# First loads issued in the order of use with waits of their own, and spare products on TensorE in the first and last passes of a fused four-layer kernel

## What is computed

```
x = L0(x, ctx, ctx)    # 16 query heads of 16, one K/V head, window mask, output product, SiLU gate, RMS norm, minus its token mean
x = L1(x, ctx, idx)    # RMS norms, 16 heads; each token sees 3 neighbours of its index; squared ReLU weights; residual
x = L2(x, ctx)         # self attention, then cross attention, 16 heads of 64, relative position bias, softmax, residuals
x = L3(x, ctx, mask)   # Mamba-2 block (in-projection, 4-tap convolution, SiLU, decayed sums, gate, RMS norm, out-projection), then 8-head cross attention
```

## Time and profile before

| what | value |
|---|---|
| median of 3 runs | 1463.18 us (1457.23 to 1464.12) |
| the profiled execution | 1463.84 us |
| its span, first to last instruction | 1462.0 us |
| TensorE (PE) busy in the span | 1306.4 us (89%) |
| VectorE (DVE), ScalarE (ACT), GpSimd (POOL) busy | 958.3, 779.8, 356.7 us |
| mean granted TensorE clock | 0.956 |
| share of TensorE, VectorE, ScalarE in the chain that ended last | 72%, 19%, 4% |

### The profile page before, as it was taken

The page is one execution under the profiler, slowest core; times in us unless marked ns, Lnnn a source line. Parts: engine busy times, 40 slices in busy tenths (PEclk is TensorE's granted clock), DMA queues, the critical chain, the costliest instruction groups (busy, mean ns, idle before and its releaser), DMA issues.

```text
span 1462.0 us, 26277 instructions
## 1 busy us (share of the span) xinstructions
PE 1306.4 (89%) x9618; PEld 1027.6 (70%) x9618; DVE 958.3 (66%) x1908; ACT 779.8 (53%) x2690; POOL 356.7 (24%) x782
## 2 busy tenths in 40 slices
PE   3667889999999999999999999999999999888755
PEld 2345667877777787778777777877787777776533
DVE  2446567768686867777686768677776868573522
ACT  1133556657565646566575656464665656464411
POOL 1112303232322213132323232131323232302020
PEclk9779999999999999999999999999999999999855
DMA  6700000000000000000000000000000000000000
GB/s 205 282 1 13 3 12 2 17 4 16 4 16 4 9 11 0 20 0 16 4 16 4 16 4 9 11 0 20 0 16 4 16 4 4 4 5 5 4 4 4
DMA packets 23967, 28.65 MB, mean 20 GB/s; under 512 B 2144, under 2 KB 20096, under 8 KB 23424
## 3 DMA queue, kind: packets, MB, share of 16 engines
q1 hardware_dynamic: 23936, 28.24, 6.0%
HBM read 26.11 MB, written 2.13 MB: 19 GB/s over the span
## 4 chain that ended last, share of the span: by engine, by line
PE 72%; DVE 19%; ACT 4%; issue 3%; SPq 1%; DMA 0%; DVEq 0%; POOL 0%; another core or an unknown queue 0%; POOLq 0%; ACTq 0%
PE psum L477 44%; PE psum L471 8%; PE psum L660 4%; DVE small_ L1002 4%; PE psum L641 3%; PE psum L581 3%; DVE sa_p L996 3%; PE psum L693 2%; PE psum L705 2%; PE psum L525 2%; ACT sa_p L798 2%; ACT A L790 2%; DVE ca_p L1010 1%; PE psum L541 1%; PE psum L737 1%
## 5 line engine op out<-in xcount | busy, mean ns | idle before, releaser
L1286 POOL TENSOR_SCALAR small_<-small_ 128x1 f32<-128x1 f32 x112 | 36.0, 321 | 946.7 <-DVE small_ L1014 477.0
L790 ACT ACTIVATE A<-A,small_ 128x128 f32<-128x128 f32 x384 | 148.5, 389 | 91.0 <-DVE small_ L1003 91.0
L471 PE MATMUL psum<-cst,A 128*128 128x128 f32 x672 | 108.8, 289 | 59.1 <-DVE A L1010 36.7
L783 ACT ACTIVATE A<-psum 128x1024 f32<-128x1024 f32 (+2 forms) x112 | 76.5, 683 | 133.6 <-PE psum L471 125.2
L471 PEld LDWEIGHTS psum<-cst,A 128*128 128x128 f32 x672 | 80.6, 147 | 80.2 <-DVE A L1010 41.7
L1175 DVE SCALAR_TENSOR_TENSOR A<-psum,half_cw,A 128x127 f32<-128x127 f32 (+2 forms) x288 | 76.3, 340 | 68.4 <-ACT A L894 68.4
L790 ACT ACTIVATE ca_p<-ca_p,small_ 128x128 f32<-128x128 f32 x256 | 98.8, 394 | 4.9 <-DVE small_ L1003 4.9
L790 ACT ACTIVATE sa_p<-sa_p,small_ 128x128 f32<-128x128 f32 x256 | 98.8, 392 | 0.1
L783 ACT ACTIVATE sa_k<-psum 128x512 f32<-128x512 f32 (+1 forms) x48 | 35.5, 739 | 98.4 <-PE psum L477 53.5
L790 ACT ACTIVATION_READ_ACCUMULATOR A<-A,small_ 128x1 f32 x384 | 72.1, 188 | 0.0
L477 PEld LDWEIGHTS psum<-sa_p,Wsaq 128*128 128x128 f32 x512 | 58.8, 193 | 18.5 <-issue 18.5
(11 more groups left out here) (219 smaller groups left out, 3281.9 us busy)
## 6 DMA issues: line engine op xcount, KB each, us to landing
inT<-in_tokT SPq DMA_DIRECT2D x16, 256.0 KB, 2.7
ctx_in<-in_ctx SPq DMA_DIRECT2D x16, 128.0 KB, 2.1
A<-bias_rows SPq DMA_DIRECT2D x1, 2048.0 KB, 9.3
Wsakv<-in_wsa_kv SPq DMA_DIRECT2D x1, 2048.0 KB, 12.3
Wcakv<-in_wca_kv SPq DMA_DIRECT2D x1, 2048.0 KB, 13.3
ctx_end<-in_tokT SPq DMA_DIRECT2D x16, 128.0 KB, 2.2
out<-x_out SPq DMA_DIRECT2D x16, 128.0 KB, 1.7
Wmi<-in_wm_in SPq DMA_DIRECT2D x1, 1288.0 KB, 18.7
```

What stands on the lines that cost most here:

```text
L471: mm = pe.transpose(out[:, c * P:(c + 1) * P], src[:, c * P:(c + 1) * P], ident)
L783: return act.activation(out, in_, ACT.Copy)
L790: ins = act.activation(p[:, h * T:(h + 1) * T], p[:, h * T:(h + 1) * T], ACT.Exp, bias=sm(part, "nm", w * HU + h, w * HU + h + 1), accum_o ...
```

## The change

- SP issues the three weights that `project0` needs right after the tokens, under a semaphore of their own, `w0_first`; the constants that VectorE's first work reads come next, then the context, then mask, setup and rel, the index, and last the two other weights of layer 0. `project0` waits for `w0_first` (three loads), `out0` for `w0_in` (now two). TensorE's wait for the six constants moves from its first instruction to `bias_table`, which stands behind `project0`. VectorE's and GpSimd's waits for the constants stay.
- `in_turn` calls a function `ahead(where, name)` ahead of each stage. On TensorE it is `spare`: it issues as many products of the identity with 256 columns of the constants as the table `SPARE` gives for this pass and stage, into a bank that this pass doesn't use; nothing reads them. They have no wait and stand ahead of the stage's own waits: 29 in the opening, 16 in the filling, 16 in the draining, 36 in the closing. In the loop and its neighbours there are none.
- The semaphores `out0_ssq` and `x1_ssq` become one, `ssq1`, that counts two for each batch (L1307, L1311); this frees one for `w0_first`.

```diff
--- before.py
+++ after.py
@@ -125,6 +125,14 @@
 }
 
 
+SPARE = {
+    "opening": {"l0_p0": 10, "l0_m0": 1, "l0_p1": 9, "l0_m1": 1, "back0": 2, "near_q": 1, "near_k": 1, "turn_o1": 4},
+    "filling": {"l0_p0": 10, "l0_m0": 1, "back0": 2, "center0": 1, "near_k": 1, "sa_m": 1},
+    "draining": {"m_hat": 2, "m_xbc": 1, "m_heads": 4, "hat3": 2, "q3": 1, "c3_p": 5, "c3_m": 1},
+    "closing": {"m_xbc": 2, "m_seg": 11, "m_xh": 1, "m_heads": 4, "m_back": 2, "hat3": 2, "q3": 1, "c3_p": 12, "c3_m": 1},
+}
+
+
 def merged(order, own, parts):
 
     rest = {k: [name for name in stages if name in own] for k, stages in PARTS.items()}
@@ -139,7 +147,7 @@
 
 NAMES = [
 
-    "const_in", "w0_in", "w1_in", "wsa_in", "late_in",
+    "const_in", "w0_first", "w0_in", "w1_in", "wsa_in", "late_in",
 
     "prep_exp", "prep_done", "bias_ps", "bias_sb", "skewed_in",
 
@@ -147,7 +155,7 @@
     "sa_hatT", "sa_q", "sa_k", "sa_v", "sa_oT", "sa_y", "ca_cT", "ca_hatT", "ca_q", "ca_k", "ca_v", "ca_oT", "ca_y",
     "m_hatT", "m_dt", "m_z", "m_xbc", "m_seg", "m_xhG", "m_y", "m_uT", "m_o", "c3_hatT", "c3_q", "c3_kv", "c3_oT", "c3_y",
 
-    "l0_osb", "gate_th", "out0_ssq", "x1_ssq", "kv1_sb", "o1T_sb",
+    "l0_osb", "gate_th", "ssq1", "kv1_sb", "o1T_sb",
     "sa_xnT", "sa_k_sb", "sa_v_sb", "sa_oT_sb", "ca_cnT", "ca_xnT", "ca_k_sb", "ca_v_sb", "ca_oT_sb",
     "m_ssq", "m_xT", "m_acc", "m_th", "m_thz", "m_u", "m_E", "m_gssq", "m_uT_sb", "c3_xnT", "c3_oT_sb",
 
@@ -329,15 +337,16 @@
                 self.next = value(1, 2)
                 self.unit = [value(2, 1), value(2, 2)]
 
-        def in_turn(eng, order, stages, restart):
-
-            def run(t, name):
+        def in_turn(eng, order, stages, restart, ahead=lambda where, name: None):
+
+            def run(t, name, where="loop"):
+                ahead(where, name)
                 for stage in stages.get(name, ()):
                     stage(t)
 
-            def phase(turns):
+            def phase(turns, where="loop"):
                 for part, name in merged(order, stages, turns):
-                    run(turns[part], name)
+                    run(turns[part], name, where)
 
             def at(b, i=None, known=None):
                 return Turn(eng, b, i, known)
@@ -345,9 +354,9 @@
             restart()
             first = at(0)
             for name in OPENING:
-                run(first, name)
+                run(first, name, "opening")
             restart()
-            phase({2: at(0), 1: at(1)})
+            phase({2: at(0), 1: at(1)}, "filling")
             run(first, "fold4")
             restart()
             phase({3: at(0), 2: at(1), 1: at(2)})
@@ -358,8 +367,8 @@
             restart()
             phase({4: at(B - 3), 3: at(B - 2), 2: at(B - 1)})
             restart()
-            phase({4: at(B - 2), 3: at(B - 1)})
-            phase({4: at(B - 1)})
+            phase({4: at(B - 2), 3: at(B - 1)}, "draining")
+            phase({4: at(B - 1)}, "closing")
 
         def need_by(eng):
             def need(t, *names):
@@ -421,16 +430,16 @@
                     sp.dma_start(dst[:], src.rearrange("(k p) n -> p k n", p=P)).then_inc(sem[name], 16)
 
             load_tokens(0)
+            weights("w0_first", [(W0k, w0_k), (W0v, w0_v), (W0q, w0_q)])
+            sp.dma_start(cst[:], consts).then_inc(sem["const_in"], 16)
+            sp.dma_start(col[:], cols).then_inc(sem["const_in"], 16)
+            sp.dma_start(row[:], rows.partition_broadcast(P)).then_inc(sem["const_in"], 16)
             load_ctx(0)
-            sp.dma_start(cst[:], consts).then_inc(sem["const_in"], 16)
+            sp.dma_start(pad_at, pad.partition_broadcast(P)).then_inc(sem["const_in"], 16)
             sp.dma_start(set_at, setup).then_inc(sem["const_in"], 16)
             sp.dma_start(rel_at, rel).then_inc(sem["const_in"], 16)
-            sp.dma_start(col[:], cols).then_inc(sem["const_in"], 16)
-            sp.dma_start(row[:], rows.partition_broadcast(P)).then_inc(sem["const_in"], 16)
             load_idx(0)
-
-            sp.dma_start(pad_at, pad.partition_broadcast(P)).then_inc(sem["const_in"], 16)
-            weights("w0_in", [(W0q, w0_q), (W0k, w0_k), (W0v, w0_v), (W0o, w0_o), (W0g, w0_g)])
+            weights("w0_in", [(W0o, w0_o), (W0g, w0_g)])
 
 
             sp.wait_ge(sem["bias_sb"], 1)
@@ -460,7 +469,6 @@
 
         @block.tensor
         def _(pe):
-            pe.wait_ge(sem["const_in"], CONSTS_IN)
             pe.sem_inc(sem["ca_cT"], 1)
             pe.sem_inc(sem["c3_kv"], 1)
             need, free, need_unit = need_by(pe)
@@ -489,6 +497,7 @@
 
 
             def bias_table(t):
+                pe.wait_ge(sem["const_in"], CONSTS_IN)
                 a = SETUP_AT["buckets"]
                 pe.matmul(Pd[0:2 * H2, 0:2 * T - 1], rel_at, set_at[0:BUCKETS, a[0]:a[1]], start=True,
                           stop=True).then_inc(sem["bias_ps"], 1)
@@ -506,7 +515,7 @@
 
 
             def project0(t):
-                pe.wait_ge(sem["w0_in"], 5 * 16)
+                pe.wait_ge(sem["w0_first"], 3 * 16)
                 pe.wait_ge(sem["tokT_in"], t.value(16, 16))
                 free(t, "x2")
                 cT = [ctxT(k) for k in range(KD)]
@@ -545,6 +554,7 @@
                 return run
 
             def out0(t):
+                pe.wait_ge(sem["w0_in"], 2 * 16)
                 need_unit(t, "l0_osb", 1)
                 product_T(Pa, W0o, 0, KD, split(q0o)).then_inc(sem["attnT"], 1)
 
@@ -768,7 +778,14 @@
                 "m_heads": [m_heads], "m_back": [m_back], "m_out": [m_out], "kv3": [kv3], "hat3": [turn3], "q3": [query3],
                 "c3_s": [scores3], "c3_p": [turn_probs3], "c3_m": [mix3], "c3_out": [project3],
             }
-            in_turn(pe, ORDER["PE"], stages, lambda: None)
+            
+            def spare(where, name):
+
+                to = {"opening": X2["ca"], "filling": X2["ca"], "draining": Pa, "closing": Pa}
+                for _ in range(SPARE.get(where, {}).get(name, 0)):
+                    pe.matmul(to[where][:, 0:D], ident, cst[:, 0:D], start=True, stop=True)
+
+            in_turn(pe, ORDER["PE"], stages, lambda: None, spare)
 
 
         @block.scalar
@@ -823,7 +840,7 @@
 
             def squares0(t):
                 need(t, "out0")
-                act.activation(junk1, Pa[:, 0:D], ACT.Square, accum_out=sm(1, "ssq")).then_inc(sem["out0_ssq"], 1)
+                act.activation(junk1, Pa[:, 0:D], ACT.Square, accum_out=sm(1, "ssq")).then_inc(sem["ssq1"], 1)
 
             def keys_values1(t):
                 need(t, "kv1", "ctx_rstd")
@@ -831,7 +848,7 @@
 
             def squares1(t):
                 need(t, "x1")
-                act.activation(junk1, x1_at, ACT.Square, accum_out=sm(1, "ssq1")).then_inc(sem["x1_ssq"], 1)
+                act.activation(junk1, x1_at, ACT.Square, accum_out=sm(1, "ssq1")).then_inc(sem["ssq1"], 1)
 
             def turned_o1(t):
                 need(t, "o1T")
@@ -1305,11 +1322,13 @@
                 ins.then_inc(sem["onehot"], 1)
 
             def rms0(t):
-                need(t, "out0_ssq")
+                need_unit(t, "ssq1", 0)
+                held()
                 rsqrt(1, sm(1, "r"), sm(1, "ssq"), 1.0 / D, 1e-6, "out0_rstd")
 
             def rms1(t):
-                need(t, "x1_ssq")
+                need_unit(t, "ssq1", 1)
+                held()
                 rsqrt(1, sm(1, "r1"), sm(1, "ssq1"), 1.0 / D, 1.1920929e-07, "x1_rstd")
 
             def pass_on(t):
```

## The result

The median of 4 runs is 1439.27 us (1438.35 to 1441.08) against 1463.10 us before; the ratio is 0.985 with a 95% interval of 0.982 to 0.988. Measured a second time, in another group of runs, the changed kernel took 1437.27 us against 1462.59, a ratio of 0.983 (0.980 to 0.986). So 24 to 25 us are gained; 28 were forecast. The profiled execution took 1438.35 us with a span of 1435.9 us, 26.1 us less than before.

The account below looks back on a forecast made before the run. Taken as bound: at both ends TensorE waits for other engines and its clock falls; the loop is nearly full. From 1463.84 us, minus 3.4 (loads), 7 (front clock) and 17.6 (tail clock), gives 1436 us; range 1428 to 1449.

Parts of the forecast that it names:

- The ceiling by b x (1 - c): Both ends: busy time b at granted clock c can give b x (1 - c); tail 24.0 us, front 16.8 us.
- Rival B: Front and tail: the clock holds everywhere, 1423 us; chance 0.07.
- The loads: Start: constants in at 12.0 us bring the first scores from 19.45 to 16.0 us, 3.4 us gained.
- The front's clock: First stretches: of 16.8 us held there, 10 us stay lost to falls and slow starts, 7 us gained.
- The tail's: Last four stretches: of 24.0 us, 6.4 us stay lost to clock falls and spares without a gap, 17.6 us gained.
- The odds of a fall: Long gaps: rests of 2.1 to 2.4 us have even odds of clock fall, over 3 us somewhat more.
- The uncovered spares: Draining: two spares ahead of `hat3` and one ahead of `m_xbc` have no idle time to cover them, 1.4 us lost.
- Rival C: Long gaps: the clock doesn't rise in them, spares at 0.87 us overrun, 13.1 us lost, 1473.5 us; chance 0.04.

## Why the prediction was right, and where its steps were off

The forecast was 1436 us in a range of 1428 to 1449, faster with 0.93. The sign, the mechanism and the size hold; the gain is 24 to 25 us where 28 were forecast. By its steps:

- **The ceiling by b x (1 - c)** held best. Rival B, the clock up everywhere, was priced at 1423 us from rows 2 and 5, a gain of 40.8 us; the kernel with 136 products, whose clock is 1.00 in the tail, takes 1423.4 us, a gain of 38.8. Of the 40.8 the clock was to give 37.4; of the 38.8 it gave some 36 to 37, if 2.0 to 2.6 us are the loads'. So the method is good to 1 or 2 us here; that the times themselves agree to 0.4 us is partly luck.
- **The loads.** The forecast was 3.4 us at the first scores within 0.7 to 3.9; the first pair of traces has 4.6 us, outside the bounds, the second 3.7 us. Two terms were mis-sized. The constants were in at 11.23 us instead of 12.0 (between 10.7 and 11.9 us in the other profiles with the new order); the wait no longer ends with the mask but with `rel`, the eleventh load, which landed 5.6 us after its issue. And the path from there to the scores takes 3.6 instead of 4.0 us, in both profiles of the changed kernel. The step that failed is the silent one, that this gain goes through to the end: 2.0 us arrive without spare products and 2.6 us with them, and the sum must take these. The two errors nearly cancel (3.4 forecast), which is luck. That the order alone doesn't give it is shown by the kernel with the old waits.
- **The front's clock:** 7 us forecast, 9.0 measured. **The tail's:** 17.6 forecast, 16.3 measured as a part of its own. Each is within 2 us.
- **The odds of a fall.** Idle rests in the five long gaps were forecast at 3.1, 2.4, 3.2, 2.1 and 2.1 us and are 2.09, 2.20, 2.98, 2.37 and 2.12 us. The first is shorter, since its products begin at half clock. In this profile a fall follows all five, two of them only behind the turn. Even odds was right over more of them: in the six profiles with the 97 products or those of one end, rests of 2.1 to 2.4 us in these five gaps were followed by half clock in 6 of 12 cases, those of 2.5 to 3.2 us in 10 of 10, those of 0.9 to 1.7 us in none of 3. The same rest is followed by a fall in one execution and not in another. In the profile of the second measurement `m_seg` stands behind the same 2.37 us as in the first and takes 1.95 us instead of 3.18:

```profile
1391.86 4.91 PE L786 MATMUL psum<-cst 128*128 128x256 f32 x22
1399.14 1.95 PE L703 MATMUL psum<-A,cst 128*128 128x512 f32 x4 [2.37 <-DVE A L1192]
```

  Long rests aren't all, though. In all five profiles with the draining's products `m_dtz` of the closing runs at half clock (4.1 to 4.6 us), while the idle times in the 9 us ahead of it are 1.7 us and less; in the kernel that spreads the others, with the same products there, it takes 2.40 us. Why is open.

  What the prediction didn't see is a gap that the change makes longer. Ahead of `m_back` in the draining the trace of before has 1.84 us; now it is 3.28 us, without spares, and the clock falls in it. Before, then the changed kernel:

```profile
1360.79 3.44 PE L705 MATMUL psum<-A 128*128 128x64 f32 x16 [2.94 <-DVE A L1195]
1366.07 1.11 PE L471 MATMUL psum<-cst,A 128*128 128x128 f32 x4 [1.84 <-DVE A L1200]
...
1346.36 2.00 PE L715 MATMUL psum<-A 128*128 128x64 f32 x16 [1.02 <-DVE A L1212]
1351.64 1.11 PE L479 MATMUL psum<-cst,A 128*128 128x128 f32 x4 [3.28 <-DVE A L1217]
1352.55 1.91 PE L479 MATMUL psum<-cst,ca_p 128*128 128x128 f32 x8
```

  `m_heads` takes 2.00 us instead of 3.44 and so ends early, while `m_gated` on VectorE, which `m_back` waits for, is done no sooner: from the start of `m_heads` to that of `m_back` it is 5.28 us in both. The turns behind it take 1.11 and 1.91 us, as at half clock before the change. The kernel with 136 products has five there and no fall.
- **The uncovered spares.** Forecast 1.4 us for the three products ahead of `hat3` and `m_xbc`. The two ahead of `hat3` take 1.0 us (1361.88 to 1362.85), the one ahead of `m_xbc` 0.4 us, both without idle time around them: as forecast.
- **Rival C** (spares at half clock overrun their gaps) is right in its price and wrong in its condition: ten in the first gap took 5.54 us of 7.6 and fourteen 7.86 us, part of it at half clock, but in both the clock had risen before the end. The argument against it, that long runs end at full speed, was too broad all the same: `m_xbc` takes 5.46 us against 2.84 in the loop, which is half clock to its end.
- **Not settled:** where half of the loads' head start goes. The idea that the clock rises later after early products isn't borne out: it first rises at 18.8 and 21.8 us in the two profiles of the changed kernel, at 24.9 and 24.0 us in those with the spare products alone. The falls come at other places in each profile, and single profiles can't tell 2 us from them.

## What to carry to other kernels

Where a pipeline fills and drains and TensorE waits for other engines in gaps of 2 to 8 us, multiply the busy time of each such stretch by one minus its granted clock: that is about what dummy products in the gaps can bring. Check the first microseconds by durations: ahead of the first rise the granted clock is shown as 1.00 here, though products take twice as long as later. Fill a gap nearly to its end, or spread the products over it; 97 products at the front of the gaps gave 24 to 25 us, the same 97 spread gave 32, and 136 gave 39. After each filling look for the gap that has grown because the work ahead of it got faster, and look at the work behind a fast turn, not only at the turn: the clock can fall right behind it.

## What was not expected of the hardware

- The clock's answer isn't to the total of idle time alone: the same number of products gained about 7 us more when the idle rest of four softmax gaps and of the taps' gap, 2 to 3 us in one piece, was cut into pieces of at most 1.3 us.
- Float32 turns hold the clock nearly as well as products (1441.5 against 1437.3 us in the median, with a wider spread).
- Products of 8 columns, whose time is their weight load (4.43 us for ten), still gained some 5 us over none.
- A load landed 1.5 to 3 us sooner after its issue with no fewer bytes ahead of it: the mask, still the ninth load, took 6.6 to 7.5 us in the three profiles with the old order and 4.5 to 5.1 us in the eleven with the new one. `rel`, moved from the fifth place to the eleventh, took 5.1 to 6.3 us instead of 3.5 to 3.6.
- In the long gaps with 97 products or those of one end, a rest of 2.5 us and more was followed by half clock every time (10 cases), one of 2.1 to 2.4 us half of the time (6 of 12).
